# A weight subtraction on GpSimd in four pieces of 256 columns in place of one of 1024

## The reference

```
x = x + xattn(layernorm(x), ctx)   # 32 heads, 8 groups of keys, 1601 keys of context
s = silu(z @ w_gate.T)             # z = layernorm(x), I = 2752 columns
s = s with the half of each row that is smallest in |s| set to 0
x = x + (s * (z @ w_up.T)) @ w_down.T
x = x + mixture(layernorm(x))      # router of 8 experts, the best 2, low-rank experts of rank 16
```

## Time and profile before

| | |
|---|---|
| median of 3 runs | 1471.86 us (1470.80 to 1472.54) |
| profiled execution | 1470.69 us, span 1469.0 us |
| TensorE busy | 1385.6 us, 94% |
| VectorE busy | 984.0 us, 67% |
| GpSimd busy | 907.6 us, 62% |
| ScalarE busy | 728.0 us, 50% |
| down projection in the span | 1121.4 to 1421.7 us |

### The profile page before, as it was taken

One profiled execution on the slowest core, in us unless ns is written; L12 is line 12 of the kernel. 1 busy time (PEld: TensorE's weight loads), 2 busy tenths in 40 slices (PEclk: granted clock), 3 DMA queues, 4 the chain that ended last, 5 costly groups with the idle time before them and its releaser, 6 DMA issues.

```text
span 1469.0 us, 30304 instructions
## 1 busy us (share of the span) xinstructions
PE 1385.6 (94%) x12775; PEld 1020.0 (69%) x12775; DVE 984.0 (67%) x1328; ACT 728.0 (50%) x919; POOL 907.6 (62%) x424
## 2 busy tenths in 40 slices
PE   3999999999999999899999969999999999999965
PEld 2555555555555555699999968888887887887842
DVE  7788888888888888830006989997961323346662
ACT  1788888888888888533227433333301111111211
POOL 0589898888888888533433413423334987887730
PEclk9999999999999999999999989999999999999987
DMA  9022333233332320124364284847357776755512
GB/s 342 2 92 91 135 114 124 98 126 107 109 106 92 106 91 17 69 78 173 116 241 184 97 273 132 278 146 253 122 198 268 239 223 209 234 175 175 163 49 88
DMA packets 111456, 217.90 MB, mean 148 GB/s; under 512 B 8321, under 2 KB 84177, under 8 KB 106321
## 3 DMA queue, kind: packets, MB, share of 16 engines
q1 hardware_dynamic: 90208, 193.34, 38.6%
q10 hardware_dynamic: 21104, 22.55, 5.1%
HBM read 173.66 MB, written 42.21 MB: 147 GB/s over the span
## 4 chain that ended last, share of the span: by engine, by line
PE 87%; DVE 6%; ACT 2%; issue 2%; DMA 1%; POOL 1%; DVEq 0%; ACTq 0%; SPq 0%
PE fast_psum L1896 17%; PE fast_psum L1788 16%; PE fast_psum L1927 16%; PE fast_psum L1806 14%; PE fast_psum L1873 13%; PE fast_psum L1825 6%; PE fast_psum L1832 1%; PE fast_psum L1910 1%; PE fast_psum L1989 1%; PE fast_psum L1954 1%; PE fast_psum L1811 1%; DMA fast_u_raw<-w_up_t 1%; DVE fast_ln_stats L98 1%; ACT fast_below L1643 1%; ACT fast_g_hi L1615 0%
## 5 line engine op out<-in xcount | busy, mean ns | idle before, releaser
L1240 DVE TENSOR_TENSOR fast_masked<-fast_psum,fast_mask_t 128x1024 f32<-128x1024 f32 (+1 forms) x416 | 488.4, 1219 | 68.3 <-PE fast_psum L1788 66.3
L1131 POOL TENSOR_TENSOR fast_pair<-fast_probs 128x1024 f32<-128x1024 f32 x192 | 457.1, 2383 | 108.0 <-ACT fast_probs L1561 49.7
L1561 ACT ACTIVATE fast_probs<-fast_masked 128x1024 f32<-128x1024 f32 (+1 forms) x416 | 437.5, 1058 | 64.8 <-DVE fast_masked L1240 49.8
L1788 PE MATMUL fast_psum<-fast_qT,fast_kraw 32*128 32x256 f32 (+1 forms) x3328 | 247.4, 403 | 1.5 <-DVE fast_masked L1240 0.8
L1806 PE MATMUL fast_psum<-fast_probs,fast_vraw 128*32 128x256 f32 (+1 forms) x3328 | 226.3, 386 | 0.8 <-ACT fast_probs L1561 0.8
L1788 PEld LDWEIGHTS fast_psum<-fast_qT,fast_kraw 32*128 32x128 f32 (+1 forms) x3328 | 154.2, 182 | 88.2 <-DVE fast_masked L1240 54.6
L1162 POOL TENSOR_TENSOR fast_g_lo<-fast_g_raw,fast_g_hi 128x2752 fp32r<-128x2752 f32 x14 | 86.1, 6151 | 143.0 <-ACT fast_g_hi L1615 120.9
L1184 POOL TENSOR_TENSOR fast_d_lo<-fast_d_raw,fast_d_hi 128x1024 fp32r<-128x1024 f32 x66 | 166.2, 2518 | 5.3
L1873 PE MATMUL fast_psum<-fast_g_hi,fast_z_hi 128*128 128x344 f32 x512 | 164.5, 321 | 2.0 <-POOL fast_g_lo L1162 2.0
L1873 PE MATMUL fast_psum<-fast_g_hi,fast_z_lo 128*128 128x344 f32 x512 | 163.3, 319 | 0.0
L1873 PE MATMUL fast_psum<-fast_g_lo,fast_z_hi 128*128 128x344 f32 x512 | 163.3, 319 | 0.0
(11 more groups left out here) (150 smaller groups left out, 1946.3 us busy)
## 6 DMA issues: line engine op xcount, KB each, us to landing
fast_d_raw<-w_down SPq DMA_DIRECT2D x63, 512.0 KB, 3.7
fast_kraw<-ctx_t SPq DMA_DIRECT2D x32, 800.5 KB, 5.8
fast_vraw<-ctx_nat SPq DMA_DIRECT2D x16, 1536.0 KB
fast_g_raw<-w_gate SPq DMA_DIRECT2D x15, 1376.0 KB, 7.2
s<-fast_res SPq DMA_DIRECT2D x16, 688.0 KB, 3.9
fast_mag<-s SPq DMA_DIRECT2D x8, 1376.0 KB, 9.8
fast_sx<-s SPq DMA_DIRECT2D x8, 1376.0 KB, 6.6
sk<-fast_sx SPq DMA_DIRECT2D x8, 1376.0 KB, 6.7
```

The costliest lines, as they stand in the source:

```text
L1131: pool.tensor_tensor(pair[:, n % PAIR_BUFS], both[:, :, 0, :], both[:, :, 1, :], ALU.add).then_inc(paired, 1)
L1240: dve.tensor_tensor(into, of, m, ALU.add).then_inc(mask_added, 1)
L1561: act.activation(probs[0:r, g % RING, hp * HALF:(hp + 1) * HALF], masked[0:r, h % SLOTS, :], ACT.Exp).then_inc(exp_done, 1)
L1788: last = pe.matmul(scores[0:r, (2 * g + hp) % SLOTS, h % 2, i * 256:(i + 1) * 256], kraw[b % BUFS][q, u, c * P:c * P + r], qT[q, b, u, :], ...
```

## The change

The subtraction of GpSimd is cut along the columns. The cast ahead of it stays whole. Only the last of the four pieces signals `d_lo_done`. Nothing else of the program differs.

```
                 pool.tensor_copy(d_hi[j][0:r, :], d_raw[j][0:r, :]).then_inc(d_hi_done, 1)
                 pool.wait_ge(d_hi_done, n + 1)
-                pool.tensor_tensor(d_lo[j][0:r, :], d_raw[j][0:r, :], d_hi[j][0:r, :].bitcast(F32),
-                                   ALU.subtract).then_inc(d_lo_done, 1)
+                for q in range(4):
+                    qs = slice(q * 256, (q + 1) * 256)
+                    last = pool.tensor_tensor(d_lo[j][0:r, qs], d_raw[j][0:r, qs], d_hi[j][0:r, qs].bitcast(F32),
+                                              ALU.subtract)
+                last.then_inc(d_lo_done, 1)
```

## The result

The changed kernel took 1467.53 us (median of 9 runs, 1466.25 to 1469.81); the kernel before, run beside it, took 1471.21 us (9 runs, 1470.17 to 1472.54). The ratio is 0.9974, with a 95% interval of 0.9966 to 0.9983: 3.7 us faster, between 2.5 and 5.0. The profiled execution took 1467.19 us, 1465.5 of them its span. Lines of `kernel.py` behind the subtraction have numbers higher by three than before.

The account below looks back on a forecast made before the run. TensorE, busy for 94% of the span, was taken as the bound, with all the room in the last group. Terms 2.8 + 1.9 + 0.35 - 1.1 = 3.95 us gave 1467.9 against the median 1471.86; range 1465.9 to 1472.7.

Parts of the forecast that it names:

- A piece costs 0.71 to 0.74 us: GpSimd's subtraction of 256 columns: 0.71 to 0.74 us, pieces following at 0.65 to 0.68, 0.35 us more a step.
- my bounds: GpSimd's extra time a step for four pieces: between nothing more (0) and 0.82 us more.
- The groups of three tiles: Down projection, 44 steps: 4.07 us of GpSimd work stays under 4.47, hidden by its 0.75 us wait; price 0.
- VectorE gets in between two pieces: GpSimd's queued pieces let waiting VectorE operations in; in step 61 the pick's operations meet pieces one by one, 2.9 us earlier.
- The rival in which it doesn't get in: Step 61: VectorE waits 2.73 in place of 2.38 us twice, 0.7 us later, about 1472.6; chance 0.14.
- the idle of 2.98 us: TensorE's wait ahead of `mix(0)`, behind step 61's pick on VectorE; 2.8 us of it was to go, between 2.0 and 2.98.
- The clock: Behind the idle, `mix(0)` and `down(61)` ran at a lowered clock; without the idle it should stay up: 1.88 us.
- The smaller place: At 1336.67 L1416 waits for a subtraction and TensorE waits 0.50 us; lock ends 0 to 0.67 earlier, taken as 0.35.
- A new wait ahead of `mix(1)`: TensorE waits for `hwt` behind `weights3` and `weight(2)`, whose five operations meet pieces or a cast: 0.7 to 1.5 us, taken as 1.1.
- what is late next: The chain to `mix(1)` through `weights3` and `weight(2)`, held up once GpSimd runs without a gap; cost taken as 1.1 us.

## Why the prediction was right

I said 1467.9 us and faster; it is 1467.53.

- **A piece costs 0.71 to 0.74 us, at a distance of 0.65 to 0.68.** The median of 264 is 0.739 us. Four took 2.82 to 3.26 us over the 66 steps, 3.02 in the median. Where VectorE doesn't get in they are 0.69 us apart (2.82 - 0.74 = 2.08, a third of it), at the upper end of what I would take as right; with one turn of VectorE of 384 columns, 0.76 on average (3.02). A step of three tiles grew by 0.42 us (3.02 against 2.60, each with one turn of VectorE), and by the groups over all 66 steps by 0.51 (3.03 against 2.52). I took 0.35, which is too low but inside my bounds: the fixed part of 0.15 to 0.19 us for each of three more pieces, without the overlap that I took off, is 0.45 to 0.57 and comes closer.
- **The groups of three tiles cost nothing.** Shown by the kernel with pieces up to step 43 (ratio 1.0000), and by GpSimd's wait of 0.32 us, which I had at 0.3 to 0.5.
- **VectorE gets in between two pieces.** In step 61 the four operations that I named meet the pieces one after another, and L1464 the cast, as written: from the start of the subtraction L1450 ends after 0.84 us (I had 0.8) and L1464 after 3.89 (I had 4.0). The rival in which it doesn't get in is out. That the idle of 2.98 us came from this collision is shown from two sides: pieces remove it, and so do waits with no piece at all.
- **The clock: 1.88 us.** It is 1.6. From the start of `mix(0)` to the next transposes it was 6.21 us before (1399.90 to 1406.11) and is 4.58 now (1397.36 to 1401.94), at a granted clock of 1.00. The direction and the cause were right, the term 0.25 us too large.
- **The smaller place: 0.35 us.** The router of step 48 starts 0.40 us earlier (15.11 to 14.71). The two profiles show 0.87 us by `multiply(61)`, but 0.56 to 0.67 of it is the chance in step 58 of the profile before, told above, with its wait of 0.33 us ahead of the router, which none of the four other kernels with whole subtractions up to step 60 has. Against them 0.20 to 0.31 us are left.
- **A new wait ahead of `mix(1)`: 1.1 us.** It is 0.97. From L1494 to the end of `weight(2)` it takes 6.01 us (1399.38 to 1405.39), where it took 3.30: 2.7 more, at the low end of my 2.6 to 3.4. Five operations are held up as I said, but not all the same five: L1480 ran free, and L1471, which has only one input in SBUF and which I had left out, was held for 0.5 us.
- **The sum.** I had 2.8 + 1.9 + 0.35 - 1.1 = 3.95 us. What the traces show is 2.98 for the idle, 1.6 for the clock, 0.3 for the smaller place and 0.97 for the new wait: 2.98 + 1.6 + 0.3 - 0.97 = 3.9 us. The distances give 3.84 at `mix(1)` against the kernel with pieces up to step 43 (83.38 to 79.54), and the medians 3.7 (2.5 to 5.0). Against the profile before the distances give 4.3, because of its chance in step 58. That the time is off by only 0.4 us is in part luck: the idle term was too small, the clock and the wait too large, and the errors nearly cancel. The gain itself was 3.95 us forecast and 3.7 measured: I counted from 1471.86, the median of three, and the nine runs beside the changed kernel gave 1471.21. The low end of my range, 1465.9, doesn't follow from its terms: all three in full and no new wait are 2.98 + 1.88 + 0.67 = 5.53 us, which gives 1466.3.

What I had wrong came out in the experiments: the price of "what is late next". In the changed kernel it is 1 us only because the pieces go on through steps 63 to 65. With whole subtractions there the kernel is over 7 us slower than with pieces, and the sign turns. Where the cut ended in the middle, the kernel was slower than before (steps 61 and 62) or no faster (44 to 60); from 61 to the end, it had the whole gain.

## What to carry to other kernels

Where TensorE waits for a row of tiny VectorE operations, look at how long they take against the same lines elsewhere, and at what GpSimd's instruction ends with them: one on 24 columns that takes 2.4 us is waiting, not working. Shorter GpSimd instructions cure it as long as GpSimd has room for their fixed cost (here 0.4 to 0.5 us of 0.75), and so does making GpSimd wait at the one or two places that matter. Then follow the chain to its next meeting with the same engine before counting the gain: a cure that stops one step too early gave back twice what it had won.

## What the runs showed of the hardware

- A `tensor_scalar` on three columns with one input in SBUF is held up too: 0.70 us beside pieces (L1471 above), 1.00 us beside a cast that ended with it (L1472), against 0.16 where GpSimd was idle. I had counted only operations with two inputs in SBUF. The Trainium skill (SBUF — State Buffer, Who interferes with whom) names `tensor_scalar` among the operations that can take the shared pair in their two-port modes; the traces agree.
- The lock works both ways. In the kernel of eight pieces L1420 of VectorE starts at 1243.38 and takes 0.57 us, as long as its neighbour L1411; the cast that GpSimd starts at 1243.48 takes 1.37 us in place of 1.04. Here VectorE had the port and GpSimd waited. Such a hand-over is paid on GpSimd's side: here 0.33 us.
- Idle times of TensorE of 0.97 and 1.30 us left the granted clock up, as did one of 2.37 us (1.98 us for the four products of `mix(0)`, with two pieces of 512), while 2.98 us was followed by a lower clock (2.56 us for the same four; granted clock 0.66), and so were 4.77 (3.27) and 4.85 (3.68). The length of the idle time alone doesn't decide it: ahead of step 44 an idle of 2.29 us, shorter than 2.37, was followed by a granted clock of 0.66 (the kernel with all casts in pieces, 1326.1 to 1331.1).
